# Square sums of the queries: squares moved past one-column selectors instead of held as the stationary operand

## The reference, cut to what matters

```python
q = (hidden_states @ Wq).reshape(B, Sq, H, D)
k = (encoder_hidden_states @ Wk).reshape(B, Skv, H, D)
v = (encoder_hidden_states @ Wv).reshape(B, Skv, H, D)
q = rmsnorm(q, gq)     # x * rsqrt(mean(square(x), axis=-1) + 1e-5) * g
k = rmsnorm(k, gk)
scores = jnp.einsum('bqhd,bkhd->bhqk', q, k) * scale
attn = jax.nn.softmax(scores, axis=-1)
out = jnp.einsum('bhqk,bkhd->bqhd', attn, v).reshape(B, Sq, H * D)
x = x + out @ Wo       # hidden_states was layernorm(x); then x + ffn(layernorm(x))
```

## Time and profile before

| | us |
|---|---|
| median of 3 runs | 1997.86 (1997.29 to 1998.62) |
| the profiled execution | 2000.24 |
| its span, first to last instruction | 1998.1 |
| busy: TensorE matmul | 1968.4 (99%) |
| busy: VectorE | 1601.0 (80%) |
| busy: GpSimd | 1154.3 (58%) |
| busy: ScalarE | 1000.3 (50%) |
| mean granted TensorE clock | 0.997 |

### The profile page before, as it was taken

The page is one execution under the profiler, slowest core; times in us unless marked ns, Lnnn a source line. Parts: engine busy times, 40 slices in busy tenths (PEclk is TensorE's granted clock), DMA queues, the critical chain, the costliest instruction groups (busy, mean ns, idle before and its releaser), DMA issues.

```text
span 1998.1 us, 34301 instructions
## 1 busy us (share of the span) xinstructions
PE 1968.4 (99%) x11532; PEld 1890.8 (95%) x11532; DVE 1601.0 (80%) x3035; ACT 1000.3 (50%) x2323; POOL 1154.3 (58%) x1305
## 2 busy tenths in 40 slices
PE   7999999999999999999999999989999999999999
PEld 6899999999999999999999999979999999999998
DVE  6877877788877778877778787888888888888875
ACT  4655555455555555555555553344444444444442
POOL 6756665533444433444332345798888888888871
PEclk9999999999999999999999999999999999999999
DMA  5434444332333332332322424110111111101001
GB/s 186 139 111 160 140 139 131 118 116 89 123 111 96 120 106 90 121 113 89 126 89 87 144 80 136 57 41 32 32 33 37 38 34 32 32 33 33 32 1 67
DMA packets 93516, 174.58 MB, mean 87 GB/s; under 512 B 13264, under 2 KB 49760, under 8 KB 91296
## 3 DMA queue, kind: packets, MB, share of 16 engines
q1 hardware_dynamic: 93344, 172.39, 26.4%
HBM read 139.00 MB, written 33.36 MB: 86 GB/s over the span
## 4 chain that ended last, share of the span: by engine, by line
PE 88%; DVE 7%; POOL 2%; ACT 2%; issue 1%; DMA 0%; SPq 0%; DVEq 0%; ACTq 0%; POOLq 0%
PE psum L409 43%; PE psum L772 19%; PE psum L442 6%; PE psum L498 3%; PE psum L475 3%; PE psum L504 3%; PE psum L483 3%; PE psum L499 3%; PE psum L551 2%; DVE ysum L1428 1%; DVE tT_lo L1185 1%; PE psum L514 1%; DVE g L1395 0%; DVE work L1291 0%; DVE g L1390 0%
## 5 line engine op out<-in xcount | busy, mean ns | idle before, releaser
L880 ACT ACTIVATE work<-psum,stats,q_rstd 100x361 f32<-100x361 f32 x256 | 163.5, 650 | 184.3 <-DVE stats L1282 184.3
L1185 DVE TENSOR_TENSOR kaT_lo<-psum,kaT_hi 128x488 fp32r<-128x488 f32 (+2 forms) x384 | 216.0, 612 | 49.0 <-ACT kaT_hi L820 49.0
L409 PE MATMUL psum<-wk,ctxT_hi 128*122 128x512 f32 x768 | 241.0, 395 | 0.0
L1844 POOL TENSOR_TENSOR inter_lo<-g,inter_hi 128x400 fp32r<-128x400 f32 x128 | 143.6, 1126 | 125.4 <-ACT inter_hi L820 124.5
L820 ACT CAST kaT_hi<-psum 128x488 fp32r<-128x488 f32 (+2 forms) x384 | 178.7, 540 | 69.7 <-PE psum L483 69.5
L1696 POOL TENSOR_SCALAR k_ss<-k_ss 122x4 f32<-122x4 f32 x192 | 37.1, 193 | 295.8 <-DVE k_ss L1241 295.0
L1698 POOL TENSOR_TENSOR k_ss<-k_ss,power 122x4 f32<-122x4 f32 x192 | 193.7, 1009 | 16.0
L1272 DVE TENSOR_REDUCE stats<-psum 100x2 f32<-100x722 f32 x128 | 115.6, 903 | 97.0 <-PE psum L442 97.0
L409 PE MATMUL psum<-inter_hi,down_hi 128*128 128x400 f32 x512 | 176.1, 344 | 3.2 <-POOL inter_lo L1844 2.0
L409 PE MATMUL psum<-inter_lo,down_hi 128*128 128x400 f32 x512 | 175.5, 343 | 0.0
L409 PE MATMUL psum<-inter_hi,down_lo 128*128 128x400 f32 x512 | 175.4, 343 | 0.0
(11 more groups left out here) (253 smaller groups left out, 6270.1 us busy)
## 6 DMA issues: line engine op xcount, KB each, us to landing
head_w<-spill_sq SPq DMA_DIRECT2D x48, 512.0 KB, 3.5
head_w<-spill_so SPq DMA_DIRECT2D x46, 512.0 KB, 3.6
wk<-spill_sk SPq DMA_DIRECT2D x12, 1024.0 KB, 5.3
wv<-spill_sv SPq DMA_DIRECT2D x48, 256.0 KB, 2.9
spill_sq<-head_w SPq DMA_DIRECT2D x16, 512.0 KB, 3.1
spill_so<-head_w SPq DMA_DIRECT2D x16, 512.0 KB, 3.0
wk_raw<-in_ctxT SPq DMA_DIRECT2D x12, 361.0 KB, 4.0
head_raw<-in_Wq SPq DMA_DIRECT2D x16, 256.0 KB, 3.8
```

The source lines that it names most:

```text
L409: last = e.matmul(out, a_, b_, start=begins and i == 0, stop=ends and i == len(passes) - 1)
L880: e.activation(attn[h][:, 0:SKV], bank[3 + h][0:SQ, 0:SKV], ACT.Exp, bias=st[:, h:h + 1], scale=rq[:, i * QH + h:i * QH + h + 1], accum_ou ...
L1185: e.tensor_tensor(dst, src, high.bitcast(F32), ALU.subtract).then_inc(S[sem], 1)
L1844: e.tensor_tensor(il[:, :], gact[n % 3][:, :], ih[:, :].bitcast(F32), ALU.subtract).then_inc(S["il"], 1)
```

## The change

For quads 1 to 15 the squares become the moving operand. A selector `select` (128 x 16, float32r) holds four stationary operands of four columns; the h-th has ones in column h and zeros elsewhere. `all_squares_summed` moves the 400 columns of each head's squares, high and low, past its selector, eight matmuls that accumulate in rows 0 to 3 of bank 3, one row a head. It stands once in a quad, in the fourth unit behind the key transposes. ScalarE copies the 4x400 sums to SBUF (`q_sums`) at the end of its unit, and TensorE, after the output product, transposes them in four pieces of 4x100 into 16 columns of bank 7 (`sums_transposed`). VectorE makes one variance of 100x16 at the start of the next quad's first unit, and GpSimd raises it in two steps, the four values of the first unit, then the twelve of the others. The squares of four heads now need four buffers. Quad 0 keeps the old way. The wait of the scores on the variance goes.

```diff
-            q_sqs = pair(a, "q_sqs", [P, GT])
+            q_sqs = [pair(a, "q_sqs0", [P, GT])]
...
+            q_sqs += [pair(a, f"q_sqs{h}", [P, GT]) for h in range(1, QH)]
+            q_sums = tensor(a, "q_sums", [QH, GT])
+            select = tensor(a, "select", [P, QH * QH], F32R)
...
 # TensorE, scores
-                        if h == 0 and u > 0 and (u - 1) % GB >= 2 and before + 1 < NQ:
-                            e.wait_ge(S["qvs"], 4 * (before + 1) + u % GB + 4 * (u % GB == 0))
...
+            def all_squares_summed(quad):
+                e.wait_ge(S["selected"], 2)
+                for h in range(QH):
+                    e.wait_ge(S["qsh"], 4 * quad + h + 1)
+                    e.wait_ge(S["qsl"], 4 * quad + h + 1)
+                    for k in range(2):
+                        last = e.matmul(bank[3][0:QH, 0:GT], select[:, cols(h, QH)], squares(quad, h)[1][k],
+                                        start=h == 0 and k == 0, stop=h == QH - 1 and k == 1)
+                last.then_inc(S["qsum"], 1)
+
+            def sums_transposed(quad):
+                e.wait_ge(S["qsev"], quad)
+                for i in range(GB):
+                    last = e.transpose(bank[7][0:SQ, GT + QH * i:GT + QH * (i + 1)], q_sums[:, cols(i, SQ)], ident[0:QH, 0:QH])
+                last.then_inc(S["qst"], 1)
...
                     query_evicted(quad, 3)
+                    e.wait_ge(S["qvs"], QH + quad)
                     value_of(quad - 1, 0, 7)
...
-                elif i in (1, 2) and more:
-                    e.wait_ge(S["ex"], 4 * u + 4)
-                    squares_summed(quad + 1, i - 1, 6)
-                    if i == 2:
-                        query_evicted(quad + 1, 1)
-                        if quad > 0:
-                            query(quad + 1, 2, 7)
+                elif i == 2 and more and quad > 0:
+                    query_evicted(quad + 1, 1)
+                    query(quad + 1, 2, 7)
...
-                    if more:
-                        e.wait_ge(S["qvs"], 4 * (quad + 1) + i)
                     e.wait_ge(S["ex"], 4 * u + 4)
                     output(quad - 1, i - 1 if more else 2 * i - 1, 6)
...
-                    e.wait_ge(S["yTl"], 2 * u + 1)
-                    squares_summed(quad + 1, i, 3)
+                    if i == 3:
+                        e.wait_ge(S["yTl"], 2 * u + 1)
+                        all_squares_summed(quad + 1)
                     query_evicted(quad + 1, i)
                     if quad > 0:
                         output(quad - 1, i, 7)
+                    if i == 3:
+                        sums_transposed(quad + 1)
...
 # ScalarE, at the end of its unit, behind the high parts of the next unit's keys
+                if i == 3 and more:
+                    e.wait_ge(S["qsum"], quad + 1)
+                    e.copy(q_sums[:, :], bank[3][0:QH, 0:GT]).then_inc(S["qsev"], 1)
...
 # VectorE
+            def query_variances(quad):
+                e.wait_ge(S["qst"], quad)
+                e.tensor_scalar(q_rstd[quad % 2][:, :], bank[7][0:SQ, GT:GT + GB * QH], 1.0 / HD, EPS, ALU.mult, ALU.add).then_inc(S["qvs"], 1)
...
-                elif u % GB == 0 and p == 0:
-                    e.wait_ge(S["qrs"], 4 * (u // GB) + 4)
+                elif u >= GB and u % GB < 2 and p == 0:
+                    e.wait_ge(S["qrs"], QH + 2 * (u // GB) - 1 + u % GB)
...
                 if n == 0:
-                    e.wait_ge(S["qss"], 4 * NQ)
+                    e.wait_ge(S["qsum"], NQ - 1)
...
+                if i == 0 and quad > 0:
+                    query_variances(quad)
                 for p in range(2):
                     maxima(u, p)
                     negated(u, p)
...
-                if i in (1, 2) and more:
-                    query_variance(quad + 1, i - 1, 6)
...
-                if i >= 2 and more:
-                    query_variance(quad + 1, i, 3)
...
 # GpSimd
+            def query_rstds(quad):
+                e.wait_ge(S["qvs"], QH + quad)
+                for i, n in ((0, 1), (1, GB - 1)):
+                    rstd = q_rstd[quad % 2][:, i * QH:(i + n) * QH].rearrange("p (i h) -> p i h", i=n)
+                    e.tensor_tensor(rstd, rstd, power[0:SQ, :].unsqueeze(1).broadcast_to([SQ, n, QH]), ALU.pow).then_inc(S["qrs"], 1)
...
+            e.tensor_scalar(select[:, :], zero[:, :], 1.0, 1.0, ALU.mult, ALU.mult).then_inc(S["selected"], 1)
+            e.wait_ge(S["selected"], 1)
+            e.tensor_scalar(select[:, 0:QH * QH:QH + 1], zero[:, 0:QH], 1.0, 1.0, ALU.mult, ALU.add).then_inc(S["selected"], 1)
...
                 if i == 0 and quad > 0:
-                    query_rstd(quad, 3)
-                if i == 3 and more:
-                    query_rstd(quad + 1, 2)
+                    query_rstds(quad)
...
-                if i in (1, 2) and more:
-                    query_rstd(quad + 1, i - 1)
```

More of the change, by code:

```diff
@@ L68 @@
 d_wv0 d_wv1 wvh wvl d_vs0 d_vs1 d_vs2 d_vs3 d_vl0 d_vl1 d_vl2 d_vl3
-q qsq qsh qsl qTh qTl qss qvs qrs
+q qsq qsh qsl qTh qTl qss qvs qrs selected qsum qsev qst
 k ksq kss kvar krs khat kTp kTh kTl
@@ L211, in build @@
         power = tensor(ctx, "power", [P, QH])
-        zero = tensor(ctx, "zero", [P, CC * (KPAD - SKV)])
+        zero = tensor(ctx, "zero", [P, QH * QH])
         ones = tensor(ctx, "ones", [P, 2], F32R)
@@ L379, in squares @@
                 return first_sq[h][:, :], [t[:, :] for t in first_sqs[h]]
-            return q_sq[:, :], [t[:, :] for t in q_sqs]
+            return q_sq[:, :], [t[:, :] for t in q_sqs[h]]
         def by_head(i, n):
@@ L651, in tensor_program @@
                 elif u == 2:
+                    query_evicted(1, 1)
                     query(1, 2, 7)
@@ L852, in query @@
                 e.wait_ge(S["qsq"], n + 1)
-                if n > QH:
-                    e.wait_ge(S["qss"], n)
+                if quad > 1:
+                    e.wait_ge(S["qsum"], quad - 1)
                 hi(sqs[0], sq, "qsh")
@@ L1855, in gpsimd_program @@
                 for t in ctxT[i]:
-                    e.tensor_copy(t[:, :, SKV:KPAD], zero[:, :].rearrange("p (c n) -> p c n", c=CC)).then_inc(const, 1)
+                    e.tensor_copy(t[:, :, SKV:KPAD], zero[:, 0:CC * (KPAD - SKV)].rearrange("p (c n) -> p c n", c=CC)).then_inc(const, 1)
                 e.memset(raw_N(i)[:, KT - 1, :], 0.0).then_inc(const, 1)
```

## The result

The changed kernel takes 1983.8 us (median of four runs, 1983.03 to 1984.19) against 1997.76 for the kernel before on the same chip: ratio 0.9929, 95% interval 0.9912 to 0.9946. The forecast was 1983.0, in a range of 1980 to 1993.5.

The account below looks back on a forecast made before the run. TensorE's queue was taken as the bound: 39.0 us of old sums go, 24.1 come, so 14.9 off the profiled 2000.24 gives 1985.3; with the median 2.4 below that execution, 1983, range 1980 to 1993.5.

Parts of the forecast that it names:

- A microsecond of TensorE is a microsecond of time: Attention stage: TensorE work counts in full as time, unless another engine is next in line.
- What goes: Quads 1 to 15: 60 groups of eight L551 products go, 55 on the path at 0.71 us: 39.0 us.
- What comes on TensorE: Per quad, eight selector products 1.46 us and four small transposes 0.40: together 1.86 us.
- Three boundaries that do not count in full: Quad boundaries set by other engines cost 1.3 (first), 0 (at 253.7) and 0.45 us (at 1134) instead of 1.86.
- The sum: 39.0 us go and 24.1 come: 14.9 us off the profiled execution, 2000.24 to 1985.3.
- First rival: GpSimd's twelve-value pow holds VectorE's negation in each quad's first unit: 4 us, 1987, or 14, 1997; chance 0.18.
- Second rival: Second unit's removed group had covered a wait for the normalisation: 10.6 us come back, 1994; chance 0.11.
- Third rival: The eight narrow selector products do not overlap: 0.34 us each gives 1999.6, 0.51 gives 2017; chance 0.06.
- Steps costed at nothing: ScalarE's copy under the output product, VectorE's one variance, both pows, and selector writes (bounded by 1 us) cost nothing.
- From the profile to the median: The median of the runs lies 2.4 us below the profiled execution, so 1985.3 becomes 1983.

Follow-up runs that it names:

- second profile of before: The kernel before the change, profiled once more with no edit: 1997.05 us.
- the high parts alone: Changed kernel with the low parts of the squares left out of the sums of quads 1 to 15: 1974.21 us.
- the long subtraction: Changed kernel with one GpSimd subtraction of 128x1200 added between the two pows of quads 1 to 14: 1987.77 us.

## Why the prediction was right

The mechanism was right and so was the largest term; the price of two boundaries and of a joint was too low by 1.9 us together. Of the forecast's own steps:

- *A microsecond of TensorE is a microsecond of time.* Shown from four sides: products doubled (+1.47 a quad), groups doubled (+0.71 each), low products left out (-0.73, but for the 0.51 that quad 3 gave back), and GpSimd's subtractions left out (nothing from quad 3 on).
- *What goes: 55 groups of 0.71, 39.0 us.* The units of the two kernels give 38.8: 30.2 in the second and third units, 0.1 in quad 0's first, and 12 x 0.71, taken from the doubled groups, in the fourth ones of ordinary quads (the groups at the three boundaries of the earlier trace rows are reckoned with these). The run with doubled groups counts 56.
- *What comes on TensorE: 1.46 + 0.40.* The products are 1.47. The transposes are 0.29, and the scores behind them 0.19 longer: 0.48 for 0.40. The forecast took its 0.40 from L551's group, whose joint it counted once, with 0.09. By units an ordinary boundary comes to 1.10 in the fourth unit, 0.05 to 0.10 in the next and the 0.71 of the fourth unit's group: at most 1.91 for 1.86.
- *Three boundaries that do not count in full.* At the first it held. From the end of the attention to the scores it took 98.16 to 100.66 in the second profile of before, and now, with the copy and its hand-overs open (0.02 + 0.49 + 0.14 us), 98.10 to 101.81; the scores of before, then the way there now:

```profile
100.66 2.20 PE psum L442 x12
```

```profile
98.10 1.25 PE psum L476 x12
99.35 1.49 PE psum L562 x8
100.84 0.02 issue
100.86 0.49 ACT q_sums L1070
101.35 0.14 issue
101.48 0.33 PE psum L569 x4
101.81 2.18 PE psum L443 x12
```

That is 1.2 more for the forecast's 1.3 (1.27 by units). At the one that the earlier trace rows has at 253.7 this step failed. I left the pow on the path there, "which keeps its place", and so costed TensorE's additions at nothing; but the change took the pow off it. In the second profile of before the chain at that place goes through GpSimd's weight splits and the pow to VectorE, and comes to TensorE only at 258.05; after, it is TensorE's alone, and the quad's first pow starts 2.0 us behind its first score instead of 3.1:

```profile
250.87 0.99 POOL q_rstd L1703
...
257.51 0.49 DVE oT_lo L1185
258.01 0.04 issue
258.05 2.45 PE psum L409 x12
```

```profile
245.93 1.98 PE psum L412 x11
247.91 0.28 PE psum L569 x4
248.20 2.17 PE psum L443 x12
250.37 6.36 PE psum L412 x30
```

GpSimd and VectorE are close behind, as the 0.51 that came back with the high parts alone shows. The kernel loses 1.78 - 0.87 = 0.91 us there (1.78 in the unit before the boundary, 0.87 gained in the one behind), in place of none, and at the last boundary, where TensorE's line now runs through too, 1.09 - 0.24 = 0.85 in place of 0.45. All 15: 1.27 + 0.91 + 0.85 + 12 x 1.91 = 25.9 us, where the forecast had 24.1.
- *The sum.* -38.8 + 25.9 = -12.9 us (-13.0 by the units) for -14.9: 1.3 of the miss are the two boundaries, 0.6 at most the joints. The medians differ by 13.8 to 14.2; the second profile of before (1997.05) lies 0.7 to 0.9 below the medians of its kernel and the changed kernel's on its own, which is most of the difference to 12.9. So the forecast of 1983 is nearer to the measured 1983.8 than its terms are to theirs, and that part is luck.
- *First rival, the second pow blocks VectorE.* Did not happen: 30 negations of 0.16 us inside it. Forced by the long subtraction, the hold makes the negation 1.17 us late and costs 4.0 for the 4 forecast, but that is chance: it does so in three quads and not in all. The Trainium skill (SBUF — State Buffer, "SBUF: two separate sides") has the shared port pair held for a whole instruction; the subtractions of these traces agree (1.33 us, to the end of one), the pows do not (0.16 us inside 2.27 and 2.48).
- *Second rival, the groups were cover.* In steady quads the second unit lost its 0.71 in full (0.69 to 0.71). Something like it happened once, in quad 0: there the second unit is 0.52 longer than in the second profile of before, and TensorE waits twice for kaT_lo in the list of waits above, where that profile has `PE psum L498 <- DVE kaT_lo L1185: 0.9, 1, 0.9`.
- *Third rival, narrow products do not overlap.* 184 ns each: no.
- *Steps costed at nothing.* The copy stays hidden where the output product lies over it; without that, 0.7 a quad, as measured. VectorE's one variance took 0.17. The second pow took 2.29 us for the 2.27 estimated, and even 2.27 more on GpSimd cost nothing. The two writes of the selectors took 0.31 and 0.23 on GpSimd, and quad 0's first unit is no longer for them (-0.08).
- *From the profile to the median.* The 2.4 us taken off fit one stretch at the lower clock level in the first unit of the profiled execution, which is 2.35 us longer by it.

## What to carry to other kernels

On a path that one engine fills, count its instructions and price them from starts: that gave 0.71 and 1.46 us as measured. Add what the group behind a small one loses, too, which the forecast had too low (0.19 measured). Do not carry the waits of the old trace over to the new one: a boundary that another engine set may become the bottleneck's own as soon as the change shortens that engine's part, so bound such places by the full price. And profile the kernel before twice when the profiled execution is off its median.

## What the runs showed of the hardware

- In this kernel a GpSimd pow of 100x12 (2.27 us) let VectorE's multiplication of 100x2 through at its 0.16 us, 30 times of 30; a GpSimd subtraction (128x400, 1.05 us; 128x1200, 2.19 us) held it to its end. The maxima, which read PSUM, ran their 0.91 us beside the long subtraction. The pows have 12 columns and the subtractions 400 and more, so whether the operation or its size makes the difference is not separated.
- A GpSimd subtraction is not in proportion to its columns: 2.19 us for 1200 with both inputs from one tile, 1.05 for 400 of three tiles.
- A stationary operand of 4 columns loads in 84 to 87 ns, one of 100 columns in 163 to 168; the products of 400 moving columns come 184 ns apart behind 4 columns and 183 behind 128.
